# Another order of sums, another engine for one product, and stores dealt over three queues at the end of a fused embedding, attention and mixture-of-experts kernel

## What is computed

```python
def _L0_ffn_ref(x, gate_w, biases, w1, w3, w2, sw1, sw3, sw2):
    xt = x.reshape(Bb * Ss, D)
    shared = jax.nn.silu(xt @ sw1) * (xt @ sw3) @ sw2
    scores = xt @ gate_w.T
    _, idx = jax.lax.top_k(scores + biases, K)          # K = 2 of E = 8 experts
    topv, _ = jax.lax.top_k(scores, K)
    p = jax.nn.sigmoid(topv)
    p = p / jnp.sum(p, axis=-1, keepdims=True)
    h = jax.nn.silu(jnp.einsum('td,edh->eth', xt, w1)) * jnp.einsum('td,edh->eth', xt, w3)
    y = jnp.einsum('eth,ehd->etd', h, w2)
    ...
    out = jnp.einsum('te,etd->td', comb, y) + shared
h = h + _L0_ffn_ref(_layernorm(h, axis=-1), ...)
```

## Time and profile before

| | |
|---|---|
| time, median of 3 runs | 258.15 us |
| lowest and highest of them | 255.88 and 260.22 us |
| the profiled execution's own time | 258.87 us |
| its span in the profile | 257.0 us |
| mean granted TensorE clock | 0.982 of full speed |
| busy share of the span: TensorE, VectorE, ScalarE, GpSimd | 91%, 74%, 61%, 44% |

### The profile page before, as it was taken

One profiled execution on the slowest core, in us unless ns is written; L12 is line 12 of the kernel. 1 busy time (PEld: TensorE's weight loads), 2 busy tenths in 40 slices (PEclk: granted clock), 3 DMA queues, 4 the chain that ended last, 5 costly groups with the idle time before them and its releaser, 6 DMA issues.

```text
span 257.0 us, 5593 instructions
## 1 busy us (share of the span) xinstructions
PE 232.6 (91%) x1491; PEld 190.6 (74%) x1491; DVE 190.0 (74%) x738; ACT 155.6 (61%) x438; POOL 114.1 (44%) x121
## 2 busy tenths in 40 slices
PE   3899989999999999988989988999999999999930
PEld 2758777878788988846675656888888888888720
DVE  3538889998979797998985867766666666665892
ACT  3056486767776676768962255666666666666390
POOL 1400000273727282822655711666666666666400
PEclk9999999999999999999997999999999999999995
DMA  6999944060707010100101521414333333348657
GB/s 200 348 353 356 328 174 167 0 239 14 233 19 239 22 42 23 41 21 13 53 32 44 133 48 41 117 52 118 85 87 83 91 92 80 98 111 239 171 134 191
DMA packets 31565, 31.68 MB, mean 123 GB/s; under 512 B 4338, under 2 KB 27419, under 8 KB 30768
## 3 DMA queue, kind: packets, MB, share of 16 engines
q1 hardware_dynamic: 27240, 24.57, 32.6%
q0 software_dynamic: 3392, 6.36, 7.6%
q10 hardware_dynamic: 904, 0.41, 0.6%
HBM read 22.80 MB, written 9.03 MB: 124 GB/s over the span
## 4 chain that ended last, share of the span: by engine, by line
PE 75%; DVE 13%; ACT 5%; issue 2%; DMA 2%; SPq 0%; DVEq 0%; ACTq 0%
PE bank L1618 15%; PE bank L1328 11%; PE bank L1638 10%; PE bank L1343 5%; PE bank L1627 5%; PE bank L1537 3%; PE bank L1522 3%; PE bank L1607 2%; PE bank L1525 2%; PE bank L1414 2%; DMA xp_both<-in_patches 2%; PE bank L1400 2%; DVE sh_h L1098 2%; PE bank L1376 2%; PE bank L1342 2%
## 5 line engine op out<-in xcount | busy, mean ns | idle before, releaser
L812 POOL DMA_INDIRECT xs_dram<-xd,pos_i x50 | 55.2, 1103 | 74.5 <-DVE pos_i L1001 61.7
L823 POOL DMA_INDIRECT y_dram<-att,goal x56 | 55.1, 985 | 37.2 <-ACT att L749 36.9
L1328 PE MATMUL bank<-wt,xp_both 128*128 128x128 f32 x288 | 40.4, 294 | 5.5 <-DMA xp_both<-in_patches 5.5
L1328 PEld LDWEIGHTS bank<-wt,xp_both 128*128 128x128 f32 x288 | 38.0, 206 | 6.9 <-DMA xp_both<-in_patches 5.8
L735 ACT ACTIVATE att<-bank 128x256 f32<-128x256 f32 x56 | 21.5, 383 | 24.4 <-PE bank L1618 24.4
L1638 PE MATMUL bank<-w_sb,att 128*128 x224 | 34.7, 277 | 0.0
L1235 DVE CAST xsT_h<-bank 128x128 fp32r<-128x128 f32 x56 | 16.3, 291 | 24.4 <-PE bank L1607 24.4
L1638 PEld LDWEIGHTS bank<-w_sb,att 128*128 128x128 f32 x224 | 29.4, 191 | 0.5 <-issue 0.2
L1618 PE MATMUL bank<-xp_both,xsT_h 128*128 x56 | 26.8, 478 | 0.7 <-DVE xsT_l L1237 0.7
L1248 DVE TENSOR_TENSOR att<-att,bank 128x256 f32<-128x256 f32 x56 | 23.0, 410 | 1.7 <-ACT att L735 1.6
L1618 PE MATMUL bank<-xp_both,xsT_l 128*128 x56 | 22.2, 396 | 0.0
(11 more groups left out here) (204 smaller groups left out, 492.3 us busy)
## 6 DMA issues: line engine op xcount, KB each, us to landing
xp_both<-in_patches SPq DMA_DIRECT2D x6, 1152.0 KB
xs_all<-xs_dram SPq DMA_DIRECT2D x56, 64.5 KB, 1.8
xd<-y_dram SPq DMA_DIRECT2D x8, 384.0 KB, 5.1
w<-in_w SPq DMA_DIRECT2D x2, 1024.0 KB, 10.9
y_dram<-att,goal POOLq DMA_INDIRECT x56, 2.6
xs_dram<-xd,pos_i POOLq DMA_INDIRECT x50
xp_both<-in_patches SPq DMA_DIRECT2D x1, 768.0 KB, 5.6
hrow<-in_txt SPq DMA_DIRECT2D x2, 384.0 KB, 7.2
```

What stands on the lines that cost most here:

```text
L812: nc.gpsimd.indirect_dma_start(out=xs_dram[:, :], out_offset=bass.IndirectOffsetOnAxis(ap=pos_i[0:rows, j, k:k + 1], axis=0), in_=xd[0:row ...
L823: nc.gpsimd.indirect_dma_start(out=y_dram[:, :], out_offset=bass.IndirectOffsetOnAxis(ap=goal[u][:, 0:1].bitcast(I32), axis=0), in_=ys[u][ ...
L1328: M(ps[:, 0:D], xp[p][:, k, :], wt[:, k, :], start=(k == 0), stop=False)
```

## The change

Everything is behind the last expert tile. (1) The slot 0 of chunk 3 (`LAST`) is scaled by ScalarE, with six instructions between `shared_silu(7, 0)` and `shared_silu(7, 1)`, and VectorE adds it with one `tensor_tensor` in the place of six fused instructions. (2) The order of the functions on VectorE and ScalarE is another one. (3) GpSimd issues the two patch stores of chunks 1 and 2, SyncE 10 stores and ScalarE 3.

```diff
@@ block.sync @@
             for turn, c in enumerate(FINISHED):
                 sp.wait_ge(fin_done, turn + 1)
-                for dst, src in out_views(c)[0::(1 if c < 2 else 2)]:
+                for dst, src in out_views(c)[:4 if c == 0 else 2 if c < 4 else 0]:
                     sp.dma_start(dst, src).then_inc(out_sent, 16)
             for u in range(U):
                 sp.wait_ge(y_sent[u], 16 * (TILES // U))
-            sp.wait_ge(out_sent, 16 * sum(len(out_views(c)) for c in range(len(CHUNKS))))
+            by_pool = sum(len(out_views(c)[2:]) for c in FINISHED[1:3])
+            sp.wait_ge(pool_sent, 16 * (2 * J + by_pool))
+            sp.wait_ge(out_sent, 16 * (sum(len(out_views(c)) for c in range(len(CHUNKS))) - by_pool))
@@ block.scalar @@
             shared_silu(EARLY + 1, 0)
+            a, b = CHUNKS[LAST]
+            act.wait_ge(y_loaded[0][LAST], 16)
+            for j in range(a, b):
+                last = A(y_rows[:, 0, j, :], y_rows[:, 0, j, :], ACT.Copy, scale=weight[:, 0, j:j + 1])
+            last.then_inc(scaled, 1)
             shared_silu(EARLY + 1, 1)
-            second_results(0)
             shared_silu(EARLY + 2, 0)
             shared_silu(EARLY + 2, 1)
-            second_results(1)
-            for c in range(2, len(CHUNKS) - 1):
+            for c in range(len(CHUNKS) - 1):
                 second_results(c)
-            for turn, c in list(enumerate(FINISHED))[2:]:
+            for turn, c in list(enumerate(FINISHED))[3:]:
                 act.wait_ge(fin_done, turn + 1)
-                for dst, src in out_views(c)[1::2]:
+                for dst, src in out_views(c)[0 if c == 4 else 2:]:
                     act.dma_start(dst, src).then_inc(out_sent, 16)
@@ block.gpsimd, behind the 56 scatters @@
+            for turn, c in list(enumerate(FINISHED))[1:3]:
+                pool.wait_ge(fin_done, turn + 1)
+                for dst, src in out_views(c)[2:]:
+                    pool.dma_start(dst, src).then_inc(pool_sent, 16)
@@ block.vector, first_results(c) @@
+                if c == LAST:
+                    dve.wait_ge(scaled, 1)
+                    V.tensor_tensor(hrow[:, a:b, :], hrow[:, a:b, :], y_rows[:, 0, a:b, :], ALU.add).then_inc(fin_first, 1)
+                    return
@@ block.vector, all_results(c) @@
-                    dve.wait_ge(scaled, c + 1)
+                    dve.wait_ge(scaled, c + 2)
@@ block.vector, the order @@
             first_results(0)
             first_results(1)
+            first_results(2)
             shared_add(EARLY)
             shared_mul(EARLY + 1, 0)
-            first_results(2)
-            shared_mul(EARLY + 1, 1)
             dve.wait_ge(sh_add, EARLY + 1)
             first_results(3)
-            all_results(0)
+            shared_mul(EARLY + 1, 1)
             shared_mul(EARLY + 2, 0)
             shared_mul(EARLY + 2, 1)
+            all_results(0)
             dve.wait_ge(fin_first, 4)
             shared_add(EARLY + 1)
+            shared_add(EARLY + 2)
             all_results(1)
-            shared_add(EARLY + 2)
             dve.wait_ge(sh_add, EARLY + 3)
```

More of the change, by code:

```diff
@@ L227, in build @@
         FINISHED = (0, 1, 2, 4, 3)
+        LAST = FINISHED[-1]
         first_loaded, second_loaded = sems("first_loaded", len(FIRST)), sems("second_loaded", 2)
@@ L260, in build @@
         raw_done, twice_done = sem("raw_done"), sem("twice_done")
-        scattered, padded, tab_done, ends_done = sem("scattered"), sem("padded"), sem("tab_done"), sem("ends_done")
+        pool_sent, padded, tab_done, ends_done = sem("pool_sent"), sem("padded"), sem("tab_done"), sem("ends_done")
         cols_done, cols_turned = sem("cols_done"), sem("cols_turned")
@@ L408, in _ @@
             sp.wait_ge(padded, 16 * (E + 1))
-            sp.wait_ge(scattered, 16 * 2 * J)
+            sp.wait_ge(pool_sent, 16 * 2 * J)
             for u in range(U):
@@ L813, in _ @@
                             out=xs_dram[:, :], out_offset=bass.IndirectOffsetOnAxis(ap=pos_i[0:rows, j, k:k + 1], axis=0),
-                            in_=xd[0:rows, j, k, :], in_offset=None).then_inc(scattered, 16)
+                            in_=xd[0:rows, j, k, :], in_offset=None).then_inc(pool_sent, 16)
             bound_reg = pool.alloc_register("bound")
```

## The result

The changed kernel takes 263.65 us (median of 4 runs, 261.89 to 266.20) against 258.96 us before: the ratio is 1.0205, with a 95% interval of 1.0157 to 1.0254. By the ratio it is slower by some 5.3 us, where 4.0 were forecast; whether it is slower by more than 2%, the interval leaves open. The 258.96 is the median of the three runs above and a fourth. The longest run, 266.20, counts as one in the chip's slower state, and the ratios in this document leave such runs out.

A forecast was written before the change was run, and what follows sets the result against it. SyncE's 13 serial stores bound the end before; afterwards GpSimd's drain would: last landing 256.4 plus 4.4 plus 0.2 gives span 261.0, plus 4.0 us, so median 258.15 + 4.0 = 262.2, range 258.0 to 265.2.

The forecast's parts named there:

- rival (a): GpSimd's final drain lasts 8.7 us from its last issue's end; span 263.6 (cheap issue) to 265.1; chance 0.28.
- the main case: GpSimd's final drain exposed with about 4 us, span 261.0, down to 260.8 with cheap issue; chance 0.47.
- the second reading: GpSimd's final drain ends 4.4 us after its last landing: 256.4 + 4.4 = 260.8.
- GpSimd's issues: GpSimd's four patch stores step about 1.27 us, starting at 250.2, the last issue ending at 255.0.
- VectorE 0.6 us later: VectorE's sums behind the last expert tile, in the new order, end at 252.6, 0.6 us later.
- the wait of 1.8 us: VectorE stands still 1.8 us behind column 7's second product, waiting for TensorE before column 8's product.
- the one of 0.75: VectorE's gap of 0.75 us before column 8's shared sum, where chunk 1's sum used to be.
- Hardware queues 1.0 us earlier: SyncE's and ScalarE's stores are done at 255.5, 1.0 us earlier than 256.5, although the sums are later.
- Rival (b): GpSimd's drain stays hidden, ending right behind the landing; span 257.2 to 258.2, not slower; chance 0.16.
- the cheap issue: GpSimd's stores step 0.58 us like SyncE's; last issue bound by chunk 2's sum; both drain readings 1.4 us less.
- Rival (c): GpSimd's store issues stretched by VectorE's sums, without a drain; last landing 257.2 to 257.9, span 258.9 to 259.6; chance 0.04.
- Rival (d): New order costs more than the dealing saves: VectorE ends at 253.7, not 252.6, span 258.2; chance 0.03.

The follow-up runs named there:

- deal_only: Kernel before with only the changed kernel's stores dealt over SyncE, ScalarE and GpSimd, sums in old order: 263.98 us, ratio 1.0197.
- sums_only: Changed kernel with the stores' lines of before, so new order of sums and ScalarE's products only: 258.60 us, ratio 1.0007.
- pool_waits: Kernel before, with GpSimd only waiting for the last sum behind its last scatter, no DMA added: 262.65 us, ratio 1.0155.
- the best version: Kernel before, old order, slot 0 of chunk 3 scaled by ScalarE, stores on three engines, GpSimd drain behind first 50 scatters: 256.54 us, ratio 0.9920.
- two_queues: Kernel before with the stores dealt over SyncE and ScalarE alone: 257.97 us, ratio 0.9977.
- the bare kernels: Computation left out but for copying texts; GpSimd issues 4 or 106 plain 64 KB stores, waits, drains: drain 382 or 8717 ns.
- early_drain: Changed kernel with one GpSimd drain between its last scatter and its first store: 259.59 us, ratio 1.0013.
- best_two_drains: The best version with another GpSimd drain behind scatter 41 of 56, amid the experts: 260.76 us, ratio 1.0055.

## Why the prediction was right, and where it was off

The engine and the wait that set the new end were forecast; how the drain's length comes about was not. The prediction named, as a sign that it was wrong, a drain "counted from the issue (then (a))", and that is what came: rival (a), at a chance of 0.28, and not the main case, at 0.47, describes the drain. That the time still came out near the forecast is luck in part: one term was 3.2 us too small and another 2.2 too large.

- **That GpSimd's drain, and not the sums or the stores, would set the end**: right, and the reason of the result. `deal_only` and `sums_only` part the two (1.0197 and 1.0007): the order alone costs nothing, and only behind the dealing it adds 0.9 us.
- **Its size**: the forecast's sum, plus 4.0 us, rested on one choice: "I take the second reading", 4.4 us behind the last landing. That was the wrong one, for a wrong reason ("a drain that waits for transfers should contain that time"): `pool_waits` shows the drain at full length with nothing under way. The term should have been 9.04 us behind the last issue: from the forecast's 255.0 that is 264.0, where 260.8 was taken, 3.2 us too early. The forecast was saved from being further off by the next error.
- **GpSimd's issues**: "I take about 1.27" for a step. Plain stores take 0.62 us each, four in 2.49; the lower bound, SyncE's 0.58, was the near one, and the scatter a bad stand-in. The last issue ended 15.3 us behind the first sum, where 17.5 (255.0 - 237.54) was forecast. With both terms put right, the forecast's sum is 15.3 + 9.04 + 0.2 = 24.5, and 24.6 was measured.
- **VectorE 0.6 us later**: 0.7 measured, with the wait of 1.8 us in its place (1.83 measured) and the one of 0.75 (0.70). In `sums_only` it costs nothing, since SyncE's queue ends later still. In the changed kernel it costs 0.9, by way of chunk 1's sum and GpSimd's last issue (see `deal_only`); the prediction did start GpSimd's stores from the moved sum (at 250.2), but put no price of its own on the move. That is why the best version has the old order.
- **Hardware queues 1.0 us earlier**: for the issue it was 1.4, for the last landing 0.2 in the changed kernel. `two_queues` has 0.9 in its tail. In the changed kernel landings were up to 2.8 us, where 2.3 was assumed.
- **Rival (a)**, 8.7 us from the last issue, had the mechanism's number. That its 263.6 for the cheap issue is also the measured median is luck: the prediction takes 1.4 us off for cheap issues, but by its own figures the last issue then starts at 252.0 and ends at 252.6, 2.4 before 255.0, and the last landing is at 254.6, 1.8 before 256.4. Rival (a) with cheap issues should have read 262.6, and the main case 260.4 and not 260.8. **Rival (b)**, a hidden drain, fell with the first row of the profile after. Its premise, though, that the 10.66 us were the leftover of the scatters and not a cost of any transfer, is what the bare kernels show: what was wrong in it is that the leftover is worked off only when the drain begins. **Rival (c)**, stretched issues, didn't show in the stores (0.60 to 0.67 us each, beside 768 wide sums with both inputs in SBUF). **Rival (d)**, a new order that costs more than the dealing saves, didn't come about as told, since VectorE ended 15.2 us behind its first sum, by the forecast's count at 252.7 and not at 253.7; what the order did cost went through GpSimd.

## What to carry to other kernels

Before work is given to an engine that had long been done, read when its program ends now and what stands at its end: here GpSimd's drain cost 82 ns for every DMA (of 128 rows, nearly all) that it had issued since its last drain, and it was invisible only while others finished later. Where GpSimd issues many DMAs, put a drain into one of its idle stretches, ahead of the part that counts, and let its last transfer be early. And in the order of a tail, keep an independent sum for each wait on another engine: with the same product on ScalarE, VectorE was done 0.7 us later than before in the new order, and 0.2 earlier in the old one, which had work for the gap (14.3 against 14.5 us behind the first sum).

## What the runs showed of the hardware

- **A drain of GpSimd is work by count**: 41 ns with no DMA since the last drain, 0.38 us with 4, 4.9 to 5.0 with 60, 8.7 with 106, 9.0 to 9.1 with 110, all counted from its begin or the last issue's end. With its own transfers still on their way a short one is longer: 2.0 us behind the last issue's end with 4 (`early_drain`), 2.5 with 19 (`best_two_drains`). The same behind plain and indirect DMAs; the number of rows in a DMA was not varied.
- **A scatter's issue can be stretched to more than twice its time, and a two-input sum on VectorE beside it is not enough for that.** GpSimd's last scatter took 2.58 us in the changed kernel, and 2.58 in `sums_only` too, where VectorE ran 18 fused sums with both inputs in SBUF in a row, in the changed kernel until 244.63; with 12 in a row, which ended as it began, it took 1.01 there and in `deal_only`. That is the direction of the rule of the Trainium skill (SBUF — State Buffer, Who interferes with whom), by which a VectorE instruction with two SBUF inputs contends with a GpSimd instruction that reads SBUF, and the indices of these indirect DMAs lie in SBUF; the earlier trace rows are another case, 1.63 against 0.96. But the two scatters before it in the changed kernel, at 240.27 and 241.59, stood beside the same row of sums and took 1.01 each, and the last one of `best_two_drains`, at 242.21 beside six such sums, took 0.98. So the traces bear the rule out in part, and what made the last scatter differ is not shown. Plain stores beside 768 wide sums took 0.60 to 0.67, against 0.53 to 0.57 on average in the bare kernels, so for them there is next to nothing of it.
